# Routed feed-forward, last stage: filler transposes, list schedule, fetch distance and tile counting

## The reference, cut to what matters

```python
gate_scores = softmax(x @ Wg + bg)              # 8 experts
topk_scores, topk_idx = top_k(gate_scores, 2)
topk_scores = topk_scores / (sum(topk_scores) + 1e-08)
for e in range(8):
    y = gelu(x @ W1[e] + b1[e]) @ W2[e] + b2[e]  # 128 -> 512 -> 128
    output += y * combine_w[..., e:e+1]
x = x + output        # x on the right is layernormed
```

## Time and profile before

| | us |
|---|---|
| median of 3 runs | 1259.83 |
| the profiled execution | 1259.69 |
| its span | 1257.7 |
| TensorE busy | 1123.3 |
| VectorE busy | 818.8 |
| ScalarE busy | 636.8 |
| GpSimd busy | 596.1 |

### The profile page before, as it was taken

The page is one execution under the profiler, slowest core; times in us unless marked ns, Lnnn a source line. Parts: engine busy times, 40 slices in busy tenths (PEclk is TensorE's granted clock), DMA queues, the critical chain, the costliest instruction groups (busy, mean ns, idle before and its releaser), DMA issues. The chain is left out here.

```text
span 1257.7 us, 31257 instructions
## 1 busy us (share of the span) xinstructions
PE 1123.3 (89%) x11462; PEld 943.9 (75%) x11462; DVE 818.8 (65%) x1780; ACT 636.8 (51%) x1143; POOL 596.1 (47%) x608
## 2 busy tenths in 40 slices
PE   6989998999999999399999999996899868999960
PEld 4776666679999877288888888885677667999960
DVE  6758997843322343378888888884688775666652
ACT  5416774434566533166666665653688421456530
POOL 4771333215666574733333334333244405567775
PEclk9989999799999999699999999998999886999995
DMA  7001211401233311100000000000111150123342
GB/s 196 10 2 35 68 50 62 181 5 56 71 79 81 116 53 31 40 2 1 0 0 0 0 0 0 0 1 3 20 21 18 28 201 17 56 75 87 82 126 63
DMA packets 59823, 60.85 MB, mean 48 GB/s; under 512 B 12528, under 2 KB 49008, under 8 KB 59216
## 3 DMA queue, kind: packets, MB, share of 16 engines
q1 hardware_dynamic: 50192, 41.71, 11.1%
q0 software_dynamic: 8640, 17.71, 5.5%
q10 hardware_dynamic: 896, 0.17, 0.1%
HBM read 41.86 MB, written 15.60 MB: 46 GB/s over the span
## 5 line engine op out<-in xcount | busy, mean ns | idle before, releaser
L1630 POOL DMA_INDIRECT f_xn<-f_xn_rows,f_source x142 | 137.0, 965 | 41.9 <-issue 40.1
L2012 PE MATMUL f_bank<-f_xT,f_w_tile 128*128 128x128 f32 x1136 | 151.0, 276 | 0.0
L2023 PE MATMUL f_bank<-f_w_down,f_hidden 128*128 x1136 | 150.2, 276 | 0.2
L2012 PEld LDWEIGHTS f_bank<-f_xT,f_w_tile 128*128 128x128 f32 x1136 | 139.2, 193 | 0.0
L2023 PEld LDWEIGHTS f_bank<-f_w_down,f_hidden 128*128 128x128 f32 x1136 | 138.5, 192 | 0.9 <-issue 0.8
L1050 POOL TENSOR_TENSOR ret_rstd<-ret_var,ret_minus_half 128x8 f32<-128x8 f32 x32 | 52.7, 1648 | 174.0 <-DVE ret_var L1089 174.0
L1641 POOL DMA_INDIRECT f_hot_row<-f_slots_y,f_slots x112 | 109.0, 974 | 33.2 <-issue 32.3
L885 PEld LDWEIGHTS a_mixed_psum<-a_v_diag,a_probT 128*64 128x64 f32 x2048 | 66.9, 140 | 60.1 <-ACT a_probT L837 43.7
L1904 ACT ACTIVATE f_w_tile<-f_w_up 128x512 f32 x142 | 87.8, 621 | 38.8 <-DVE f_owner L1806 36.9
L747 POOL TENSOR_TENSOR X<-X,a_mixed 128x128 f32<-128x128 f32 x64 | 29.3, 457 | 159.3 <-DVE a_mixed L780 158.8
L788 DVE TENSOR_REDUCE a_top<-a_scores 128x16 f32<-128x1024 f32 x64 | 78.4, 1225 | 35.4 <-PE a_scores L870 34.4
(11 more groups left out here) (300 smaller groups left out, 2818.1 us busy)
## 6 DMA issues: line engine op xcount, KB each, us to landing
f_slots_y<-f_y_out SPq DMA_DIRECT2D x70, 128.0 KB, 2.2
a_v_rows<-in_ctx SPq DMA_DIRECT2D x16, 256.0 KB, 3.9
f_xn_rows<-f_xn SPq DMA_DIRECT2D x16, 256.0 KB, 13.6
f_w_up<-in_f_up SPq DMA_DIRECT2D x1, 2560.0 KB, 8.9
f_w_down<-in_f_down SPq DMA_DIRECT2D x1, 2560.0 KB, 16.8
f_xn<-f_xn_rows,f_source POOLq DMA_INDIRECT x142, 2.5
X<-in_x SPq DMA_DIRECT2D x4, 512.0 KB, 6.7
kv_ctxT<-in_ctxT SPq DMA_DIRECT2D x8, 256.0 KB, 5.7
```

The source lines that it names most:

```text
L1630: pool.indirect_dma_start(out=x_in[:, s % RING, :], out_offset=None, in_=xn_rows[:, :], in_offset=bass.IndirectOffsetOnAxis(ap=source[:, s ...
L2012: last = pe.matmul(bank_h[m % 3][:, j * P:(j + 1) * P], w_tile[m % W_RING][:, j * P:(j + 1) * P], xT[m % 3][:], start=True, stop=True)
L2023: last = pe.matmul(bank_y[m % 2][:, 0:D].unsqueeze(1), hidden[m % 3][:, j, :], w_down[:, bass.ds(expert + E0, 1), j, :], start=(j == 0), s ...
```

## The change

Four edits concern the last stage alone: `WARM_COUNT` goes from 88 to 120; the second lists stand at steps 0, 2, 4, 6, and the rest of the list is read at step 8; `ahead` is (8, 24); `added_at` is (53, 58, 64, 69). The three operations that normalise the softmax scores move from behind the owners to ahead of `sources_first`. One edit concerns both feed-forward stages: full tiles are counted by adding 127 to the count of the last part, casting to integers, shifting right by 7 and casting back; the table of bounds and its load are gone.

```diff
-                seq(dve.tensor_tensor(over[:], count[:].unsqueeze(3).to_broadcast(shape),
-                                      tile_bounds[:].unsqueeze(1).to_broadcast(shape), ALU.is_gt))
-                seq(dve.tensor_reduce(full[:].rearrange("p k e -> p e k"), over[:], AXIS.X, ALU.add))
+                seq(dve.tensor_scalar(count[:, :, parts - 1], count[:, :, parts - 1], float(P - 1), None, ALU.add))
+                seq(dve.tensor_copy(count_int[:], count[:]))
+                seq(dve.tensor_scalar(full_int[:], count_int[:], 7, None, ALU.logical_shift_right))
+                seq(dve.tensor_copy(full[:].rearrange("p k e -> p e k"), full_int[:]))
...
                 dve.tensor_reduce(tile_owner[:], ended[:], AXIS.X, ALU.add).then_inc(S["owner_column"], 1)
+                if spec["kind"] == "softmax":
+                    seq(dve.tensor_reduce(rec[:], score[:], AXIS.X, ALU.add))
+                    seq(dve.reciprocal(rec[:], rec[:]))
+                    seq(dve.tensor_tensor(score[:], score[:], bc(rec), ALU.mult))
                 sources_first()
...
                 else:
-                    seq(dve.tensor_reduce(rec[:], score[:], AXIS.X, ALU.add))
-                    seq(dve.reciprocal(rec[:], rec[:]))
-                    seq(dve.tensor_tensor(score[:], score[:], bc(rec), ALU.mult))
                     total(weight[0], score, first)
...
-WARM_START, WARM_COUNT, WARM_BETWEEN, WARM_UP = 28, 88, 6, 24
+WARM_START, WARM_COUNT, WARM_BETWEEN, WARM_UP = 28, 120, 6, 24
...
-    added_at=(52, 57, 62, 68), hot_later=(2, 6, 10, 14), listed=16, ahead=(8, 20)
+    added_at=(53, 58, 64, 69), hot_later=(0, 2, 4, 6), listed=8, ahead=(8, 24)
```

More of the change, by code:

```diff
@@ L1485, in ffn_phase @@
         rank, before, all_ones = sb("rank", [P, EXPERTS]), lent("before", [P, P]), lent("all_ones", [P, P])
-        tile_bounds, tile_numbers = lent("tile_bounds", [P, parts, TILES]), sb("tile_numbers", [P, M])
+        tile_numbers = sb("tile_numbers", [P, M])
         segment_table = sb("segment_table", [P, 4 * EXPERTS + 1])
@@ L1492, in ffn_phase @@
         ones_row, per_tile, running = (lent(k, by_expert) for k in ("ones_row", "per_tile", "running"))
-        over = lent("over", [P, EXPERTS, parts, TILES])
+        count_int, full_int = (sb(k, [P, EXPERTS, parts], I32) for k in ("count_int", "full_int"))
         count, full = sb("count", [P, EXPERTS, parts]), sb("full", [P, parts, EXPERTS])
@@ L1533, in ffn_phase @@
         loads = [(gate_w[:], dram[spec["gate_w"]]), (gate_b[:], dram[spec["gate_b"]].to_broadcast([P, EXPERTS])),
-                 (rank[:], dram["rank"]), (before[:], dram["before"]), (tile_bounds[:], dram["tile_bounds"][:, 3 - parts:3, :]),
-                 (tile_numbers[:], dram["tile_numbers"]), (segment_table[:], dram["segment_table"]), (row_numbers[:], dram["row_numbers"]),
+                 (rank[:], dram["rank"]), (before[:], dram["before"]),                  (tile_numbers[:], dram["tile_numbers"]), (segment_table[:], dram["segment_table"]), (row_numbers[:], dram["row_numbers"]),
                  (token_rows[:], dram["token_rows"])]
@@ L1710, in _ @@
                                       before_it[:].unsqueeze(2).to_broadcast(per_count), ALU.subtract))
-                shape = [P, EXPERTS, parts, TILES]
-                seq(dve.tensor_tensor(over[:], count[:].unsqueeze(3).to_broadcast(shape),
-                                      tile_bounds[:].unsqueeze(1).to_broadcast(shape), ALU.is_gt))
-                seq(dve.tensor_reduce(full[:].rearrange("p k e -> p e k"), over[:], AXIS.X, ALU.add))
+                seq(dve.tensor_scalar(count[:, :, parts - 1], count[:, :, parts - 1], float(P - 1), None, ALU.add))
+                seq(dve.tensor_copy(count_int[:], count[:]))
+                seq(dve.tensor_scalar(full_int[:], count_int[:], 7, None, ALU.logical_shift_right))
+                seq(dve.tensor_copy(full[:].rearrange("p k e -> p e k"), full_int[:]))
                 seq(dve.tensor_copy(until[:, 1::parts, :], full[:, 0::parts - 1, :]))
@@ L2041, in ffn1 @@
 def ffn1(g):
-    ffn_phase(g, "f1", dict(kind="softmax", plus_xn=False, part_tiles=(16, 8, 8), last=True, shared=0, following=None, added_at=(52, 57, 62, 68), hot_later=(2, 6, 10, 14), listed=16, ahead=(8, 20), more_rows=1, gelu=ACT.Gelu_apprx_tanh,
+    ffn_phase(g, "f1", dict(kind="softmax", plus_xn=False, part_tiles=(16, 8, 8), last=True, shared=0, following=None, added_at=(53, 58, 64, 69), hot_later=(0, 2, 4, 6), listed=8, ahead=(8, 24), more_rows=1, gelu=ACT.Gelu_apprx_tanh,
                             gate_w="L1_ffn_Wg", gate_b="L1_ffn_bg", w_up="f1_up", w_down="f1_down",
@@ L2095, in launch_inputs @@
         "before": np.triu(np.ones((P, P), np.float32), 1),
-        "tile_bounds": np.tile(P * np.arange(TILES, dtype=np.float32) + np.float32([[P - 1], [P - 1], [0]]), (P, 1, 1)),
         "segment_table": np.concatenate([np.tile(np.where(np.arange(4 * EXPERTS) % EXPERTS == EXPERTS - 1, 1 - EXPERTS, 1),
```

## The result

The changed kernel has a median of 1243.88 us (1240.97 to 1244.77, four runs) beside 1259.67 for the kernel before (1258.69 to 1261.57): ratio 0.9865, 95% interval 0.9843 to 0.9886, or 15.8 us. Forecast were 1244.5 and 15.2 us.

A forecast was written before the change was run, and what follows sets the result against it. GpSimd's queue was taken as the bound, the first gather's start setting the end: 1151.6 + 80.2 + 11.05, less 0.4, a span of 1242.5; with 2.0 around it 1244.5 us, own range 1241 to 1248.5 (60%).

The forecast's parts named there:

- Part 1: Counting by shifts: last stage's first list product can start 1.1 us earlier; 0.4 us taken in the third layer.
- Part 2: 32 more fillers ahead of the last stage's first lists keep full clock; source list read 9.0 us earlier, counting included.
- Rival (a): Full clock is lost as the last stage's first lists begin: 1252.4 us, chance 15%.
- Part 3: Second lists at steps 0, 2, 4, 6: first gather at R+103.7, R being the source list's reading; 4 us for clock.
- Rival (c): First lists lose full clock and second lists keep TensorE at half until step 8: slower, 1264.0 us, chance 3%.
- (b): The ramp, the tile loop's first steps, keeps full clock: 4 us less, 1240.5 us, chance 13%.
- (d): GpSimd's own pace bounds and its starts cannot move; only the list stage's 9.0 and third layer's 0.4 remain: 1250.3, 7%.
- Part 4: Longer fetch distance on GpSimd: value 0, bounds 0 and 3 us gained, since 4 us of slack would hide shorter waits.
- Part 5: Rows added a step later: VectorE no longer waits for group 0's gathers; the 80.21 and 11.05 us stay.

The follow-up runs named there:

- Experiment 1: The kernel before with 120 fillers instead of 88, nothing else: median 1253.68 us.
- experiment 2: The changed kernel with 88 fillers again, all its other edits kept: median 1250.85 us.
- experiment 6: The changed kernel without the six fillers between the first lists: median 1246.07 us.
- experiment 4: The changed kernel with 18 more filler transposes on TensorE ahead of each of the first two second lists: median 1241.85 us.
- experiment 3: The kernel before with the four settings alone (place of second lists, list read at 8, `ahead`, `added_at`): median 1255.53 us.
- Experiment 7: The changed kernel with `ahead` (8, 20) and `added_at` (52, 57, 62, 68) as before: median 1244.56 us.
- experiment 10: The kernel before with the counting by shifts in the third layer alone: median 1258.61 us.
- experiment 8: The kernel before with the counting by shifts and the moved score operations alone, 88 fillers and old settings: median 1254.04 us.

## Why the prediction was right, point by point

**The bound** was the queue of GpSimd from the first gather on: 80.21 us before, 79.73 after, and a tail of 11.1 and 11.2. What set the end was the start of the first gather in every trace. That it would change hands, to the stores and so to TensorE, is shown by the 4.32 us wait.

**Part 1**, the counting: 1.1 us forecast, 1.16 measured at the first list. In the third layer 0.4 was taken, the wait of its first list, and 0.6 measured (14.9 instead of 15.5 from `prefix` to the list). What the prediction did not see is that the counting and the fillers depend on each other. Experiment 1 has the fillers without it, and loses the level in the profiled execution: 1.5 us from `prefix` to the end, where the fillers are worth 7.5 on the changed kernel (experiment 2). The medians do not show this dependence (6.9 and 7.0).

**Part 2**, the fillers: forecast 9.0 us for both parts, measured 35.16 - 25.85 = 9.3. "Kept" was argued from the gate section alone, as no thinner work. The runs bear it out in all six traces that have 120 fillers, the shorter counting and the six between. In these traces it holds only with two conditions that I had not stated: a short gap ahead of the lists (0.74 and 0.15 us held, 1.84 and 4.09 did not), and the fillers between the lists (experiment 6). Rival (a) is what experiment 2 shows; its 1252.4 stands beside 1250.85.

By the rule of the Trainium skill (TensorE: Matmul & The Clock Gate, "Part 4: PE-mode transpose") the number of fillers could not have mattered. The 7.55 us between the changed kernel and experiment 2, which differ in 32 transposes and nothing else, contradict it here.

**Part 3**, the walk of the ramp: tile 8 at R+32.3 with the 4 us for the clock, measured R+32.55; the first gather at R+103.7, measured R+105.0. The half level lasted 10 us (5 to 12 expected). Priced at 4 us, experiment 4 took 3.0 of it back, with a piece of 3.4 us at half left. Rival (c) is out, since in no trace was the ramp at half until tile 8; (b) is out by the 10 us at half, and (d) by the first gather, which came 4.5 us earlier from the source list. That the four settings pay by themselves is shown by experiment 3, by 2.6 to 4.2 us in the traces; the second lists' place alone was not run. Of the 1.3 us missing, 1.0 lies between tile 43's transpose (R+98.9, forecast 98.6 with the 4 us) and the first gather: 6.1 instead of 5.1, a stretch that was summed from four rows and sized too small.

**Part 4** is the step that was wrong. The fetch distance was priced at 0, because its waits would be hidden by 4 us of slack. Experiment 7 shows 2.7 us in the trace, of which an estimated 1.5 is the fetch distance. The slack was there (5.9 us between the last fetch at R+99.1 and the first gather), but with (8, 20) the fetches ended 7.3 us later, not 2 to 3. Behind the two waits the queue is 3.1 us late: each lot waits for one tile more, at 1.9 us, and the lost level adds 1.2. The seven later lots, which wait for transposes again, add 4.2; the prediction had them run without a gap. The bound "3 gained" contains both sizes, so the sum was not hurt; the edit did its part by keeping the fetches hidden. Experiment 7 also changes `added_at`; since group 0's rows are fetched behind the last fetch, that cannot have moved the first gather.

**Part 5** holds: the gathers run on past groups 3, 4 and 6 without a pause.

**The sum** in the trace: 9.3 from the lists, 4.5 from the first gather (5.8 forecast), 0.5 from the gathers, less 0.1 in the tail: the 14.2 us of the last stage, and 0.6 from the third layer. The medians say 15.8. The remaining 1 us is within what executions differ by: held against experiment 10's trace of before's last stage, the last stage alone is 15.3 us shorter. That the median came within 0.6 us of the forecast is in part luck, since the smaller gain ahead of the first gather (1.3 less) is made up by 0.3 from the lists, 0.3 net behind the first gather and 0.2 in the third layer, and by the 1 us that no part accounts for.

**What stays open.** The medians of single parts (7.0 for the counting, 5.1 for the settings, 7.0 for 134 fillers) add up to more than the whole, while the traces' 1.5, 2.9 and 7.6 add up to 12.0 of 14.2. For the counting, the profiled execution has the other 5 us ahead of the last stage, 2.7 of them ahead of the third layer, where no edit can have caused them. The granted clock, averaged over a whole run, fits that: its median is 0.946 in the runs of experiment 8 and 0.942 in the 16 of before beside them, in which faster runs have the higher clock (0.942 to 0.945 in the four fastest, 0.936 to 0.938 in the four slowest). Why the clock is higher in experiment 8 stays open.

## What to carry to other kernels

When an engine's queue is the bound, look for the event that lets its last unbroken run begin, and walk the path to that event; here two thirds of the gain came from a stage 100 us ahead of it. Filler work that holds the clock should reach up to the work it is for: price the idle gap that it leaves, and look whether an edit that shortens the wait also closes that gap. Keep a second trace of an unedited stage, since it shows how far two traces differ with no edit between them. And before calling a setting worthless because slack hides it, sum all of its waits against that slack.

## What the runs showed of the hardware

- Busy time alone does not hold TensorE's clock. Lists back to back, 3.90 us busy of 4.10, were followed by half level, while the same lists with six transposes between them stayed at full for 9 us.
- A product list 40 wide took 1.88 to 1.95 us at full clock and 3.47 at half (experiment 2): the full clock is worth 1.8 times on narrow products too.
- In the 14 traces the third layer began between 207.6 and 211.6 us after the start, with no edited instruction ahead of it: 4 us of scatter that a single trace carries into every later time.
